# Local attention: inverse lengths as a power of minus one half on GpSimd in place of ScalarE's root and VectorE's reciprocal

## What is computed

```python
def l2norm(t):
    return t / jnp.maximum(jnp.linalg.norm(t, axis=-1, keepdims=True), 1e-12)

def attn_layer(x, Wqkv, qs, ksc, Wo):
    qkv = x @ Wqkv
    q, k, v = jnp.split(qkv, 3, -1)        # each as 16 heads of 64
    q = l2norm(q) * qs
    k = l2norm(k) * ksc
    q = q * cos * scale + rotate_half(q) * sin * scale
    k = k * cos * inv + rotate_half(k) * sin * inv
    out = local_attention(q, k, v)         # windows of 32, each sees itself and the one before
    return out @ Wo
```

## Time and profile before

| what | value |
|---|---|
| median of 3 runs | 5636.39 us (5633.79 to 5652.36) |
| profiled execution | 5639.38 us |
| its span | 5637.6 us, mean granted clock 0.946 |
| PE, DVE, ACT, POOL busy | 4852.8, 3790.4, 3198.8, 1906.2 us |

### The profile page before, as it was taken

One profiled execution on the slowest core, in us unless ns is written; L12 is line 12 of the kernel. 1 busy time (PEld: TensorE's weight loads), 2 busy tenths in 40 slices (PEclk: granted clock), 3 DMA queues, 4 the chain that ended last, 5 costly groups with the idle time before them and its releaser, 6 DMA issues. The chain is left out here.

```text
span 5637.6 us, 167378 instructions
## 1 busy us (share of the span) xinstructions
PE 4852.8 (86%) x74160; PEld 2833.7 (50%) x74352; DVE 3790.4 (67%) x4626; ACT 3198.8 (57%) x3838; POOL 1906.2 (34%) x1342
## 2 busy tenths in 40 slices
PE   7868887996888599988998899979998799889997
PEld 4523333443333266645665466636664466536663
DVE  5657772334777488847886588748884688658884
ACT  4536663222666477735775477636774577546773
POOL 1320000003000155505553355515551455325560
PEclk9979998997999899999999999989999999999998
DMA  0011110002111111101111011101111111101111
GB/s 24 11 63 39 35 35 30 0 0 64 34 34 40 45 37 39 36 32 36 37 40 44 22 39 36 36 32 37 39 36 35 32 36 40 47 18 39 36 40 39
DMA packets 96672, 196.92 MB, mean 35 GB/s; under 512 B 27312, under 2 KB 45872, under 8 KB 93872
## 3 DMA queue, kind: packets, MB, share of 16 engines
q1 hardware_dynamic: 95920, 185.86, 12.8%
HBM read 64.13 MB, written 15.73 MB: 14 GB/s over the span
## 5 line engine op out<-in xcount | busy, mean ns | idle before, releaser
L1499 POOL TENSOR_TENSOR part_of_local<-part_of_local,sine_of_local 128x512 f32<-128x512 f32 x768 | 960.2, 1272 | 1062.2 <-DVE sine_of_local L1436 1062.2
L897 ACT ACTIVATE prob_of_ca<-ps 128x1024 f32<-128x1024 f32 (+3 forms) x768 | 596.6, 813 | 332.1 <-PE ps L771 231.6
L1506 POOL TENSOR_TENSOR part_of_local<-part_of_local,inverse_of_local 128x1024 f32<-128x1024 f32 x384 | 722.1, 1902 | 144.1 <-DVE inverse_of_local L1468 144.1
L1473 DVE TENSOR_REDUCE total_of_local<-prob_of_local 128x16 f32<-128x1024 f32 x192 | 234.3, 1220 | 415.7 <-ACT prob_of_local L1412 415.7
L1433 DVE TENSOR_TENSOR part_of_local<-ps,rope 128x1024 f32<-128x1024 f32 x384 | 466.7, 1215 | 46.4 <-ACT square_of_local L1380 46.4
L789 PE MATMUL ps<-keys_of_ca,queries_of_ca 64*128 64x512 bf16 (+3 forms) x1536 | 335.1, 346 | 184.0 <-DVE top_of_ca L929 68.8
L1272 PE MATMUL ps<-qkv,shifted 128*128 128x512 f32 x768 | 396.3, 639 | 84.9 <-POOL values_of_local L1509 79.7
L1436 DVE TENSOR_TENSOR sine_of_local<-ps,rope 128x1024 f32<-128x1024 f32 x384 | 466.5, 1215 | 0.0
L1282 PE MATMUL ps<-qkv,shifted 128*128 128x512 f32 x768 | 383.2, 622 | 73.7 <-ACT heads_out_of_local L1408 60.0
L1358 PEld LDWEIGHTS ps<-prob_t_of_local,mixed_of_local 64*64 64x64 f32 x12288 | 341.0, 134 | 161.3 <-issue 150.3
L1367 PE MATMUL ps<-heads_out_of_local,wo 128*128 128x128 f32 x3072 | 392.3, 283 | 14.4 <-ACT heads_out_of_local L1408 14.0
(11 more groups left out here) (198 smaller groups left out, 9798.5 us busy)
## 6 DMA issues: line engine op xcount, KB each, us to landing
mixed_of_local<-values_of_local SPq DMA_DIRECT2D x636, 128.0 KB
mixed_of_local<-values_of_local SPq DMA_DIRECT2D x264, 64.0 KB
queries_of_ca<-q_parts SPq DMA_DIRECT2D x384, 32.0 KB
keys_of_ca<-k_parts SPq DMA_DIRECT2D x384, 32.0 KB
qkv<-in_qkv SPq DMA_DIRECT2D x7, 1536.0 KB, 6.3
rope<-in_rope SPq DMA_DIRECT2D x7, 1024.0 KB, 8.8
q_parts<-parts_of_ci SPq DMA_DIRECT2D x16, 384.0 KB, 2.5
k_parts<-parts_of_ci SPq DMA_DIRECT2D x16, 384.0 KB, 2.5
```

Of the source, the lines that this page charges most:

```text
L897: nc.scalar.activation(prob[:, i % 2, 2 * two:2 * two + 2, j:], ps[:, 2 * two:2 * two + 2, j:], ACT.Exp, scale=scale).then_inc(raised, 1)
L1499: nc.gpsimd.tensor_tensor(out, out, sine[:, side, :, (1 - to) * half:(2 - to) * half], ALU.add).then_inc(rotated, 1)
L1506: nc.gpsimd.tensor_tensor(part[:, t % 2, side], part[:, t % 2, side], by, ALU.mult).then_inc(scaled, 1)
```

## The change

The root on ACT and the reciprocal on DVE go. `length` (the sums of squares) is bounded below by 1e-24 in place on DVE (`guard`), now between the lengths and rotate_k, and POOL raises it to the power -0.5 with a tensor of constants, between its rotations and its scalings. The buffer `root` and the semaphore `rooted` go; a small buffer `minus_half` is filled once a stage by a third memset on POOL, ahead of the two others, and the waits for `cleared` count it. The sums now also wait until an earlier tile's inversion has read the buffer.

```diff
--- before.py
+++ after.py
@@ -1199,7 +1199,7 @@
         part = st.sb("part", [P, 2, 2, HEADS, DH])
         sine = st.sb("sine", [P, 2, HEADS, DH])
         length = st.sb("length", [P, 2, 2 * HEADS])
-        root, inverse = st.sb("root", [P, 2, 2 * HEADS]), st.sb("inverse", [P, 2, 2 * HEADS])
+        minus_half, inverse = st.sb("minus_half", [P, 2 * HEADS]), st.sb("inverse", [P, 2, 2 * HEADS])
         queries = st.sb("queries", [P, PAIRS, P])
         keys = st.sb("keys", [P, PAIRS, WIN + L])
         prob = st.sb("prob", [P, PAIRS, 2, DH])
@@ -1213,7 +1213,7 @@
         q_made, k_made, v_made = st.sem("q_made"), st.sem("k_made"), st.sem("v_made")
         q_turned, k_turned, scored = st.sem("q_turned"), st.sem("k_turned"), st.sem("scored")
         p_turned, weighed, projected = st.sem("p_turned"), st.sem("weighed"), st.sem("projected")
-        q_squared, k_squared, rooted = st.sem("q_squared"), st.sem("k_squared"), st.sem("rooted")
+        q_squared, k_squared = st.sem("q_squared"), st.sem("k_squared")
         q_out, k_out, raised = st.sem("q_out"), st.sem("k_out"), st.sem("raised")
         p_out, o_out, v_out = st.sem("p_out"), st.sem("o_out"), st.sem("v_out")
         q_parts, k_parts, summed = st.sem("q_parts"), st.sem("k_parts"), st.sem("summed")
@@ -1243,7 +1243,7 @@
             def _(sp):
                 for dst, src in fetches:
                     sp.dma_start(dst, src).then_inc(fetched, 16)
-                sp.wait_ge(cleared, 2)
+                sp.wait_ge(cleared, 3)
                 for t in range(NT):
                     r = t % RING * 2
                     sp.wait_ge(v_out, t + 1)
@@ -1368,7 +1368,7 @@
                                                 start=p == 0, stop=p == PAIRS - 1)
                     last.then_inc(projected, 1)
 
-                pe.wait_ge(cleared, 2)
+                pe.wait_ge(cleared, 3)
                 steps((make_q, 0), (make_k, 0), (turn_q, 1), (project, 3), (turn_k, 1), (turn_p, 2), (score, 1),
                       (make_v, 0), (weigh, 2))
 
@@ -1382,10 +1382,6 @@
                 def square_k(t):
                     act.wait_ge(k_made, t + 1)
                     nc.scalar.activation(square[:, 1], by_head(KEY_SLOT), ACT.Square).then_inc(k_squared, 1)
-
-                def roots(t):
-                    act.wait_ge(summed, 2 * t + 2)
-                    nc.scalar.activation(root[:, t % 2], length[:, t % 2], ACT.Sqrt).then_inc(rooted, 1)
 
                 def out_q(t):
                     act.wait_ge(q_turned, t + 1)
@@ -1419,7 +1415,7 @@
                     nc.scalar.activation(values[:, t % RING * 2:t % RING * 2 + 2], by_head(VALUE_SLOT).rearrange(
                         "p (a h) d -> p a h d", a=2), ACT.Copy).then_inc(v_out, 1)
 
-                steps((square_q, 0), (square_k, 0), (out_q, 1), (out_k, 1), (out_p, 2), (roots, 0), (out_v, 0),
+                steps((square_q, 0), (square_k, 0), (out_q, 1), (out_k, 1), (out_p, 2), (out_v, 0),
                       (raise_p, 1), (out_o, 2))
 
             @block.vector
@@ -1444,6 +1440,7 @@
 
                 def lengths(t):
                     dve.wait_ge(q_squared, t + 1)
+                    wait_past(dve, inverted, t - 1)
                     nc.vector.reduce_sum(length[:, t % 2, 0:HEADS], square[:, 0], AX_X).then_inc(summed, 1)
                     dve.wait_ge(k_squared, t + 1)
                     nc.vector.reduce_sum(length[:, t % 2, HEADS:], square[:, 1], AX_X).then_inc(summed, 1)
@@ -1461,11 +1458,9 @@
                                             top[:, :].rearrange("p (h n) -> p h n", h=2).unsqueeze(3)
                                             .to_broadcast([P, 2, PAIRS, DH]), ALU.subtract).then_inc(shifted, 1)
 
-                def invert(t):
-                    dve.wait_ge(rooted, t + 1)
-                    nc.vector.tensor_scalar(root[:, t % 2], root[:, t % 2], 1e-12, None, ALU.max).then_inc(guarded, 1)
-                    dve.wait_ge(guarded, t + 1)
-                    nc.vector.reciprocal(inverse[:, t % 2], root[:, t % 2]).then_inc(inverted, 1)
+                def guard(t):
+                    dve.wait_ge(summed, 2 * t + 2)
+                    nc.vector.tensor_scalar(length[:, t % 2], length[:, t % 2], 1e-24, None, ALU.max).then_inc(guarded, 1)
 
                 def totals(t):
                     dve.wait_ge(raised, t + 1)
@@ -1485,7 +1480,7 @@
                     dve.wait_ge(projected, t + 1)
                     nc.vector.tensor_tensor(cur[:, tokens(t)], cur[:, tokens(t)], two_banks(OUT_SLOT)[:, 0, 0:P], ALU.add).then_inc(added, 1)
 
-                steps((rotate_q, 0), (lengths, 0), (rotate_k, 0), (maxima, 1), (shift, 1), (invert, 0), (add, 3),
+                steps((rotate_q, 0), (lengths, 0), (guard, 0), (rotate_k, 0), (maxima, 1), (shift, 1), (add, 3),
                       (totals, 1), (even, 1))
                 dve.wait_ge(added, NT)
 
@@ -1499,15 +1494,22 @@
                         nc.gpsimd.tensor_tensor(out, out, sine[:, side, :, (1 - to) * half:(2 - to) * half],
                                                 ALU.add).then_inc(rotated, 1)
 
+                def invert(t):
+                    if t == 0:
+                        pool.wait_ge(cleared, 3)
+                    pool.wait_ge(guarded, t + 1)
+                    nc.gpsimd.tensor_tensor(inverse[:, t % 2], length[:, t % 2], minus_half[:, :], ALU.pow).then_inc(inverted, 1)
+
                 def scale(t, side, rotated, scaled):
                     pool.wait_ge(rotated, 2 * t + 2)
                     pool.wait_ge(inverted, t + 1)
                     by = inverse[:, t % 2, side * HEADS:(side + 1) * HEADS].unsqueeze(2).to_broadcast([P, HEADS, DH])
                     nc.gpsimd.tensor_tensor(part[:, t % 2, side], part[:, t % 2, side], by, ALU.mult).then_inc(scaled, 1)
 
+                nc.gpsimd.memset(minus_half[:, :], -0.5).then_inc(cleared, 1)
                 nc.gpsimd.memset(keys[:, :, 0:WIN], 0.0).then_inc(cleared, 1)
                 nc.gpsimd.memset(values[:, 2 * RING - 1], 0.0).then_inc(cleared, 1)
-                steps((lambda t: rotate(t, 0, q_parts, q_rotated), 0), (lambda t: rotate(t, 1, k_parts, k_rotated), 0),
+                steps((lambda t: rotate(t, 0, q_parts, q_rotated), 0), (lambda t: rotate(t, 1, k_parts, k_rotated), 0), (invert, 0),
                       (lambda t: scale(t, 0, q_rotated, q_scaled), 0), (lambda t: scale(t, 1, k_rotated, k_scaled), 0))
 
 
```

## The result

| what | before | after |
|---|---|---|
| median | 5635.96 us (5633.79 to 5652.36) | 5940.17 us (5936.93 to 5944.17) |
| span of the profiled execution | 5637.6 us | 5935.1 us |
| its mean granted clock | 0.946 | 0.932 |
| 28 rounds of a stage (make_q of tile 3 to that of tile 31), sum of the six stages | 2519.0 us | 2761.6 us |

The ratio is 1.0542, with a 95% interval of [1.0525, 1.0559] (so bracketed throughout): the changed kernel is 304 us slower, and the prediction of 5525 us, with its range to 5790, was wrong. Of the 304 us, 243 lie in the 168 rounds (16.44 us each on the mean, in place of 14.99) and some 60 at the starts and ends of the stages, 10 each.

A forecast was written before the change was run, and what follows sets the result against it. PE, nearly full, was taken as the bound: 168 rounds by 0.76 us is 128, less 7 for late tiles, less 10 at stage ends, 111; 5639.4 less 111 less 3 gives 5525 us, range 5502 to 5790.

The forecast's parts named there:

- rival A: POOL's long power sets the round, (25.46 + P) / 2 beyond P = 2.86 us; chance 0.06 to P = 3.7, 0.29 beyond.
- PE's own round of 14.16 us: Local attention: PE, nearly full, has an undisturbed round of 14.16 us against 14.92, 0.76 us a tile.
- the gap of 0.44: PE's idle time before make_k, waiting for ACT's copy L1408; 0.44 us, said not to be the true price.
- ACT's loads go, make_k is free: ACT loses root and both table loads; L1408 ends in time for make_k, with 0.2 to 0.3 us of cover.
- rival C: The table loads stay because another function in the loop wants another table; 5640 to 5660 us, chance 0.02.
- DVE, "isn't next, but it is near": DVE's wait before the totals shrinks by the load; rotate_q could start at 2116.13, against 2116.31 set by make_q.
- The guard, 0.30 us, hidden by 0.2: On DVE ahead of rotate_k: takes 0.30 us, and DVE is ready 0.2 us before the scores.
- the path of two rounds: From turning queries to doing so two tiles later, via DVE and POOL: 25.46 + P us within 28.32.
- Rival B: Another wait replaces the removed one, as a guard waiting for POOL's rotation; round 14.5, 5590 us, chance 0.12.
- The power, 1.9 us taken, 0.3 to 5.4 as bounds: P, its length on POOL between rotate_k and scalings: taken as one scaling's price, free up to 2.86 us.
- The ends, 2.15 less 2P for each stage: Gain at each stage's start and end, memset included; at P = 1.9, 1.65 us lost, 10 in six.
- The upper end of the range, 5790: Slowest time allowed, at P = 5.5, close to the upper bound of the power.

The follow-up runs named there:

- experiment 5: Kernel before without ACT's root, reciprocal of the row totals written to PSUM: 5499.39 us; the same PSUM edit alone on the kernel before: 5632.03 us.
- Experiments 1 and 2: First: experiment 1. Second: the changed kernel with a product in place of the power on POOL, 5614.69 us.
- experiment 3: Changed kernel with the power only for the queries' 16 lengths and a product for the keys' 16: 5704.05 us.
- the fillers: Changed kernel with extra, unused products on PE ahead of turn_q's wait in every tile: eight 5880.78 us, four 5870.08 us.
- experiment 1: Kernel before without the root on ACT and its table loads, inversion on DVE taking the sums: 5592.23 us.
- experiment 6 with both edits: Changed kernel, power kept, with the reciprocal of the row totals and the sums of squares both in PSUM: 5792.17 us.

## Why the prediction was wrong, step by step

The forecast of 5525 us was 415 us short, in three parts. The power was put at 1.9 us and takes 5.44: rival A's formula with this P gives 5636 + 141 = 5777, which is 252 us of the 415. The collisions of DVE and POOL, which no term of the sum has, are 134. The remaining 29 is what the formula itself lacks where nothing collides. The power's term alone would have left the time within the range to 5790; the collisions took it out.

- **What bounds before, and PE's own round of 14.16 us**: right. Most rounds of experiment 5 are 14.16 to 14.2, and its 168 rounds are 120 us shorter than those of before, where 168 by 0.76 less the late tiles promised 121. Reading the price from an undisturbed tile, and not from the gap of 0.44, held.
- **ACT's loads go, make_k is free**: right; rival C fell with the 564 instructions that ACT no longer has.
- **DVE, "isn't next, but it is near"**: this step failed. It moved the totals and the evening forward by the 1.28 us of the load and kept their durations. The rows on which it stood show the scalings ending as the evening begins; an operation that is moved must be priced beside its new neighbours. The missing term is 1.4 us on DVE (1.23 to 2.58 or more), 83 us of the 123. Experiments 1 and 2 show it, with no power and with one of 0.25 us.
- **The guard, 0.30 us, hidden by 0.2**: the term was mis-sized, 0.60 in the mean and 1.32 at worst, and it is on the path of two rounds, which had it at 0.30. Rival B named just this (a guard that waits for POOL's rotation); it came on top of A and not in its place.
- **The power, 1.9 us taken, 0.3 to 5.4 as bounds**: the term was mis-sized by 3.5 us, and its upper bound, 5.4, was met by luck: no run shows passes, and experiment 3 has the cost as 0.158 us for each element. I took the value nearest to the other POOL rows, all of them products and sums, which say nothing of a power. With two ends 18 times apart and the free room at 2.86, the upper end should have had more weight than 0.29.
- **The formula of rival A**: right in form. It puts P = 5.44 at 141 us over before, and 170 was measured where nothing collides. The collisions, with what they set off, add 134 us to that. Of that the guard and the scalings lie on the path of two rounds: 0.41 and 0.18 us, 0.3 a round, some 50 us. The rest goes with the alternation, PE's wait and the lower clock; the fillers gave 56 us back. How the rest divides is open: the fillers moved the collisions as well, and fillers together with the PSUM edits were not tried.
- **The ends, 2.15 less 2P for each stage**: at 5.44 it gives 8.7 us lost, measured were about 10.
- **The upper end of the range, 5790**: it had P = 5.5 with every other cover intact. Rivals that need the same neighbour to be busy don't exclude each other, and a range must add them.

A sentence on the neighbour. Beside POOL's scalings the evening takes 2.70 us with two SBUF operands and 1.22 with one of them in PSUM. The Trainium skill (Advanced Engine Details and Errata, GPSIMD Details) says that POOL shares a read and a write interface with DVE, and conflicts with DVE's instructions that are in a 2-port perf mode or have two SBUF inputs. The trace agrees for the evening, which has two, beside the scalings, and not beside the power (below). The guard has one SBUF tile as input and one as output; it takes up to 1.32 us beside POOL's rotation, and 0.19 with its input in PSUM. Whether it ran in such a mode no view here shows. One input and one output in SBUF is not enough for it: the reciprocal of the totals has them too, and takes 0.25 us in all 186 tiles of experiment 1 where it lies beside the scalings. Read beside the rows of before, the page would have pointed to the failed step.

By the ratio of 1.96 that the prediction quoted from the Trainium skill (GPSIMD Engine Reference, Performance versus the Vector engine) the power was 0.69 us. The trace says 5.44, so for a power it doesn't hold; the estimate of 4.3 us from the same page's section Performance pitfalls for Q7 kernels was nearer.

## What to carry to other kernels

When an engine gives a gap back, its successors move, and each must be priced beside what it then lies next to, above all a DVE operation on two SBUF tiles beside POOL's products and sums; the cheapest cure here is one small operand in PSUM. An operation on an engine whose trace has nothing of its kind is measured first, or placed where the engine is idle, ahead of the wait and not behind it: the same 5.44 us cost 293 us in one place of POOL's plan and 43 in the other (5792 and 5542, against 5499 in experiment 5, which has no power and leaves out the root). A path of k rounds with a free room in it is worth writing down as a formula; it was 29 us off at twice the free room for which it was made.

## What the runs showed of the hardware

- The power on POOL takes 5.44 us for 128x32 and 2.91 for 128x16, so 0.158 us for each element of a partition and 0.38 to start; a product of 128x32 takes 0.25. It is the power that is dear, 21 times the product.
- The power itself slows nothing on DVE: in after the evening at 2127.53 lies wholly beside it and takes 1.22 us (the row stands in the result), as do all 96 evenings that lie beside the power alone (1.22 to 1.23), while the scalings take it to 2.70 in experiment 1.
- DVE's colliding operation does not run slower, it waits for the end of POOL's instruction: 180 of the 186 evenings of experiment 1 that begin inside a scaling end 1.08 us after it, however much of it was left (most often 1.6 us), and 161 of the 186 guards of after that begin inside a rotation or scaling end 0.04 us after it. 22 of the other 25 guards began just before it ended and waited for the next one too.
- The collision costs both: POOL's scaling has a mean of 2086 ns in after, at most 2889, and 1903 without.
- A wait of the same length did not always bring the clock down. In after it fell to 0.50 behind 46 of the 78 waits of 1.5 us or more at turn_q, and turn_q to make_q then took 12.4 us on the mean, against 10.63 in the short round shown; in experiment 6 with both edits it fell behind 6 of 48 such waits. What was expected of the fillers, 0.50 after every such wait, said too much.
